# Top-k attention on one core: an exact mask line, a looped exact search, and part of the bound test moved to GpSimd

## The chip, the cores and the metric

The kernel runs on one core of a Trainium2 chip. The core has five engines that run side by side and meet through semaphores: TensorE (PE; its weight loads are shown as PEld), VectorE (DVE), ScalarE (ACT), GpSimd (POOL) and the queue engine SP. The metric is the time of one execution on the device, in microseconds (us), as the median of several runs.

## The reference, cut to what matters

Four layers follow each other on x of shape 32 x 256 x 128: attention a, a mixture of experts, attention b, the experts again. Only attention a is touched. It has 16 heads of width 8, and each query keeps its 76 largest scores of 256:

```python
topk = max(1, int(Tx * 0.3))                       # 76
scores = jnp.einsum('bhid,bhjd->bhij', q, k) * scale
topk_scores, indices = jax.lax.top_k(scores, topk)
masked = jnp.full_like(scores, -jnp.inf)
masked = masked.at[bi, hi, ti, indices].set(topk_scores)
attn = jax.nn.softmax(masked, axis=-1)
out = jnp.einsum('bhij,bhjd->bhid', attn, v)
```

That is 32 x 16 x 256 = 131,072 rows of 256 scores, and in each the 76th largest value has to be found.

## The kernel before, in words

**Groups and steps.** The work of attention a is cut into 64 groups of 8 heads (two groups per sequence). A group is 16 tiles of 128 queries x 256 keys, held in SS, which has room for four groups. The engines run steps: in step t, group t is counted, group t-1 is searched, and groups t-2 and t-3 are masked, turned, exponentiated and weighed. A step has eight slots, one per head. Four steps are unrolled in the body of a hardware loop (`schedule`).

**Finding the 76th value.** ScalarE counts, three times over all 16 tiles, how many scores of a row lie above a threshold (`count`, line 792: an activation with Sign and an accumulator). After each of the first two counts GpSimd moves the threshold (`move`, lines 474 to 476); after the third it writes the upper bound hi_t (line 496) and kk, the place of the wanted value below that bound (line 498). VectorE then, for each head (`largest`, lines 919 to 942), zeroes the values above hi_t (line 928, two operations on two tiles), takes the 8 largest (933), removes them (937) and takes the next 8 (941). That gives 16 sorted values per row, in L. `picks` (lines 944 to 973) reads mid, the value in place kk, and nxt, the one after it.

**The mask line.** The cut is set half-way between mid and nxt, times 1e15 (lines 961 and 966). ScalarE writes relu(cut - 1e15 x score) into gone (`outsiders`, line 768), which is large for what has to go. The two values count as apart only if mid x (1 - 2^-20) is above nxt (line 963).

**The exact search.** A row fails if kk is not in 1 to 15, if the largest value found isn't below the bound, if mid is not positive, or if mid and nxt are not apart. TensorE adds the failures of each tile over its rows (`judged`), and VectorE reads the sums (`check_flags`, lines 990 and 992, in slot 3). If any is over zero, `redo` goes through 16 unrolled copies of a search, one per tile: each reads the flag of its tile, and branches past the copy if it is zero; otherwise ten rounds of MAX8 and MATCH_REPLACE8 run on that tile (lines 1049 to 1055). If none is over zero, one branch goes past all 16 copies. After that VectorE signals okay (line 994).

**What waits for okay.** GpSimd's differences of group t-2 (line 488: scores minus their maximum, scaled, into ring, two tiles for each head), and ScalarE's outsiders of that group. TensorE turns ring and gone together (`turn`, lines 637 and 638), and ScalarE exponentiates the result (line 778).

**GpSimd's own order in a step.** hi_t and kk; differences of heads 6, 7 of group t-3; in even steps the reciprocal deviation of the next sequence; the first move; the wait for okay; differences 0, 1, 2 of group t-2; the second move; in odd steps `guess` (line 454, a power over 32 columns, and lines 456 and 457); differences 3, 4, 5; in even steps a copy of the values (line 517). VectorE evacuates the scores of group t+1 into SS in the same step (`evac`, line 913), takes the sums for the normalisation (`normalise`, line 982), and masks a Gram matrix (line 876).

Of the kernel before, what the change touches and what calls it, by code (L numbers as in the profile page):

```python
# [4 lines left out]
BATCH, T, D = 32, 256, 128  # L5
P = 128
HALVES = T // P
# [48 lines left out]
def build(nc, x, W_qkv, b_qkv, W_out, b_out, Wq, Wk, Wv, Wp, pos, gate_w, gate_bias,  # L56
# [7 lines left out]
    with ctx:  # L64
        def sb(name, shape, dt=f32):
            return ctx.enter_context(nc.sbuf_tensor(name, shape, dt))
# [43 lines left out]
        mlast = sb("mlast", [P, HALVES, 8])  # L110
        nb = sb("nb", [P, 2, HALVES])
        work = sb("work", [P, HALVES, T])
# [221 lines left out]
        zt = ab("zt", [P, 2, T])  # L334
        vraw = ab("vraw", [P, HALVES * H, HD])
# [19 lines left out]
                      "diff out pused pt pv on own aown pown slow oc gate pgate upper vput ini inid")  # L355
# [74 lines left out]
        with nc.Block() as block:  # L430
            @block.gpsimd
            def _(pool):
# [31 lines left out]
                def step(t, b, u):  # L464
# [373 lines left out]
            def _(dve):  # L838
# [55 lines left out]
                def step(t, b, u):  # L894
# [24 lines left out]
                    def largest(lag, p, between):  # L919

                        if not runs(t, lag):
                            return
                        z, y = (u - lag) % 4, (u - lag + 1) % 2
                        if own.n:
                            own.need(own.n)
                        for i in range(2):
                            c = 2 * p + i
                            n = own.mark(V.scalar_tensor_tensor(zt[:, i, :], SS[:, z, c, :], hi_t[:, y, c:c + 1], SS[:, z, c, :],  # L928
                                                                ALU.is_le, ALU.mult))
                        next(between, None)  # L930
                        for i in range(2):
                            own.need(n - 1 + i)
                            m = own.mark(V.max(L[:, y, 2 * p + i, 0:8], zt[:, i, :]))
                        next(between, None)
                        for i in range(2):
                            own.need(m - 1 + i)
                            n = own.mark(V.match_replace(zt[:, i, :], L[:, y, 2 * p + i, 0:8], zt[:, i, :], GONE))
                        next(between, None)
                        for i in range(2):
                            own.need(n - 1 + i)  # L940
                            m = own.mark(V.max(L[:, y, 2 * p + i, 8:16], zt[:, i, :]))
                        next(between, None)

                    def picks():
# [91 lines left out]
                def redo(dve, V, z):  # L1036
# [4 lines left out]
                    with dve.If(any_failed > 0):  # L1041
                        for c in range(GT):
                            failed = dve.value_load(flags[0:1, c:c + 1], min_val=0, max_val=P)
                            with dve.If(failed > 0):
                                slow.n = 0
                                src = SS[:, z, c, :]
                                w = work[:, 0, :]
                                for r in range(TOPK // 8 + 1):
                                    slow.link(V.max(mx[:, 0, :], src if r == 0 else w))
                                    if r == TOPK // 8:  # L1050
                                        slow.link(V.memset(mx[:, 0, TOPK % 8:8], GONE))
                                    slow.link(V.match_replace(w, mx[:, 0, :], src if r == 0 else w, GONE))
                                slow.link(V.tensor_scalar(w, w, GONE_BELOW, -FAR, ALU.is_gt, ALU.mult))
                                slow.link(V.tensor_tensor(src, src, w, ALU.add))
                                slow.link(V.memset(cut[:, z, c:c + 1], -0.5 * FAR * STEEP))
# [812 lines left out]
```

## Time and profile before

| | |
|---|---|
| median of 3 runs | 5771.29 us (5760.17 to 5799.41) |
| profiled execution, its own time | 5762.57 us |
| span of that execution in the trace | 5760.7 us |
| attention a in the trace | about the first 3000 us |
| busy over the span | PE 89%, DVE 72%, ACT 62%, POOL 32% |
| mean granted TensorE clock | 0.889 |

The profile is one execution. A share over the whole span mixes four layers, so the stage has to be read by windows. "Idle before" is time in which the engine ran nothing ahead of an instruction, with what released it: another engine's line, or "issue" where the profile shows no wait. Clock is the granted share of TensorE's full speed.

### The profile page before, as it was taken

What the parts mean: (1) busy time and instruction counts of PE and PEld (TensorE: products, weight loads), DVE (VectorE), ACT (ScalarE), POOL (GpSimd) and SP (SyncE); (2) the same over time, 40 slices, a digit from 0 to 9 for tenths busy, and PEclk for the clock granted to TensorE, in tenths of its full rate; (3) what the DMA queues carried; (4) which work ended last, traced back from release to release, by engine and by line L of the source; (5) the groups of instructions that cost most, each with busy time, mean ns of one, the idle gap of its engine ahead of it and who ended that gap; (6) DMA issues with size and microseconds to landing.
All of it is one profiled execution on the core that took longest, in us unless ns stands there. A gap on an engine that the chain in (4) does not pass through costs nothing. (4 is left out here: it accounts for less than half of the span.)

```text
span 5760.7 us, 127365 instructions
## 1 busy us (share of the span) xinstructions
PE 5131.6 (89%) x36862; PEld 3785.5 (66%) x36862; DVE 4153.1 (72%) x14778; ACT 3573.5 (62%) x11201; POOL 1843.7 (32%) x3026
## 2 busy tenths in 40 slices
PE   5788899899878898999888999989999999899998
PEld 3455566566545565655557888877666667788887
DVE  3777687887777888778867888865555555688886
ACT  3777688888777888888872222227767777222222
POOL 1223232332223233233324444441111111344444
PEclk6677788887788889788889999999999999999999
DMA  2000000000000000000003444430000000334434
GB/s 59 1 1 2 2 2 1 1 2 2 2 2 2 2 2 2 2 2 1 1 1 75 89 83 80 89 61 12 10 12 10 11 10 10 75 76 86 88 75 103
DMA packets 199731, 165.26 MB, mean 29 GB/s; under 512 B 47971, under 2 KB 195974, under 8 KB 199046
## 3 DMA queue, kind: packets, MB, share of 16 engines
q1 hardware_dynamic: 199046, 157.32, 13.4%
q8 instruction: 284, 4.65, 0.3%
q14 instruction: 401, 3.28, 0.2%
HBM read 146.52 MB, written 10.49 MB: 27 GB/s over the span
## 5 line engine op out<-in xcount | busy, mean ns | idle before, releaser
L792 ACT ACTIVATE junk<-SS,nt 128x256 bf16<-128x256 f32 x3072 | 1516.2, 502 | 20.9 <-DVE SS L913 17.5
L1256 ACT ACTIVATE f_th<-bank 128x256 f32<-128x256 f32 x1088 | 416.9, 383 | 1148.5 <-PE bank L1187 1148.5
L1156 POOL TENSOR_TENSOR f_hid<-f_g_m,f_cbs 128x256 f32<-128x256 f32 x1024 | 743.6, 726 | 852.3 <-DVE f_g_m L1401 630.8
L637 PE MATMUL bank<-ident,ring 128*128 128x128 f32 x4096 | 914.2, 350 | 37.8 <-issue 27.6
L637 PEld LDWEIGHTS bank<-ident,ring 128*128 128x128 f32 x4096 | 739.9, 226 | 269.9 <-issue 215.5
L1186 PE MATMUL bank<-f_xTf,wgT 128*128 128x256 f32 x2176 | 693.1, 400 | 52.7 <-DVE f_g_m L1401 39.1
L488 POOL TENSOR_SCALAR ring<-SS,nmx 128x256 f32<-128x256 f32 x1024 | 524.0, 512 | 592.7 <-DVEq L994 438.2
L1802 DVE TENSOR_REDUCE nmxb<-bank 128x2 f32<-128x512 f32 x512 | 329.5, 686 | 476.0 <-PE bank L1574 476.0
L928 DVE SCALAR_TENSOR_TENSOR zt<-SS,hi_t 128x256 f32<-128x256 f32 x1024 | 478.9, 508 | 255.3 <-issue 241.1
L650 PE MATMUL bank<-pT,vaug 128*32 128x256 f32 x2048 | 643.7, 446 | 11.2 <-ACT pT L778 8.5
L1187 PE MATMUL bank<-f_xTf,wuT 128*128 128x256 f32 x2176 | 651.4, 381 | 0.0
L1218 PEld LDWEIGHTS bank<-wdT,f_hid 128*128 128x128 f32 x4096 | 601.5, 191 | 67.3 <-POOL f_hid L1156 13.2
L1218 PE MATMUL bank<-wdT,f_hid 128*128 128x128 f32 x4096 | 629.5, 276 | 10.4 <-POOL f_hid L1156 10.3
L792 ACT ACTIVATION_READ_ACCUMULATOR junk<-SS,nt 128x1 f32 x3072 | 602.2, 196 | 0.0
L768 ACT ACTIVATE gone<-SS,cut 128x256 bf16<-128x256 f32 x1024 | 464.0, 505 | 155.3 <-DVEq L994 130.0
L609 PE MATMUL bank<-k,q 8*128 8x256 f32 x2048 | 531.4, 455 | 19.5 <-DVE SS L913 14.3
L1393 DVE SCALAR_TENSOR_TENSOR f_g_s<-f_th,bank 128x256 f32<-128x256 f32 x1088 | 451.4, 415 | 106.9 <-ACT f_th L1256 87.2
L1401 DVE TENSOR_TENSOR f_g_m<-f_g_s,bank 128x256 f32<-128x256 f32 x1088 | 456.3, 419 | 75.2 <-POOL f_hid L1156 0.4
L638 PE MATMUL bank<-minus,gone 128*128 128x128 bf16 x2048 | 498.4, 243 | 0.0
L1693 ACT ACTIVATE probb<-bank,nmxb 128x256 f32<-128x256 f32 x1024 | 440.5, 494 | 78.1 <-DVE nmxb L1802 77.6
L778 ACT ACTIVATE pT<-bank 128x512 f32<-128x512 f32 x512 | 300.9, 589 | 292.4 <-PE bank L638 291.9
L609 PEld LDWEIGHTS bank<-k,q 8*128 8x128 f32 x2048 | 314.6, 213 | 249.4 <-issue 161.2
(234 smaller groups left out, 8603.2 us busy)
## 6 DMA issues: line engine op xcount, KB each, us to landing
f_cbs<-f_shares SPq DMA_DIRECT2D x512, 256.0 KB, 5.9
qrow<-q_rows SPq DMA_DIRECT2D x512, 8.0 KB
q_rows<-qTb SPq DMA_DIRECT2D x32, 128.0 KB, 2.0
out_dram<-xres SPq DMA_DIRECT2D x4, 1024.0 KB, 9.3
f_shares<-f_combT SPq DMA_DIRECT2D x64, 32.0 KB, 1.5
px<-pext SPq DMA_DIRECT2D x16, 15.8 KB
nat<-in_L_attn_a_W_qkv_dram SPq DMA_DIRECT2D x3, 64.0 KB
bqk<-in_L_attn_a_b_qkv_dram SPq DMA_DIRECT2D x8, 0.1 KB
```

Source lines behind the costliest of these rows:

```text
L488: last = pool.tensor_scalar(ring[:, h % 4, i, :], SS[:, (u - lag) % 4, c, :], nmx[:, (u - lag) % 4, c:c + 1], DOWN, ALU.add, ALU.mult)
L609: last = nc.tensor.matmul(S[h % 3][:, i * T:(i + 1) * T], q4[r, par, g // 4, i * P:(i + 1) * P], k4[r, par, g // 4, :], start=True, stop=True)
L637: nc.tensor.matmul(o, ring[:, h % 4, i, k * P:(k + 1) * P], ident[:, :], start=True, stop=False)
L638: last = nc.tensor.matmul(o, gone[:, h % 4, i, k * P:(k + 1) * P], minus[:, :], start=False, stop=True)
L650: last = nc.tensor.matmul(O[PAD32 * (h % 4):PAD32 * (h % 4 + 1), (h // 4) * T:(h // 4 + 1) * T], vaug4[:, v // 2, k, 8 * (v % 2) + h, :], ...
L768: last = nc.scalar.activation(gone[:, h % 4, i, :], SS[:, v, c, :], ACT.Relu, bias=cut[:, v, c:c + 1], scale=-STEEP)
L792: nc.scalar.activation(junk[:, c % 2, :], SS[:, uu % 4, c, :], ACT.Sign, bias=bias(c), accum_out=acc[:, k, uu % 4, c:c + 1]).then_inc(s["s ...
L928: n = own.mark(V.scalar_tensor_tensor(zt[:, i, :], SS[:, z, c, :], hi_t[:, y, c:c + 1], SS[:, z, c, :], ALU.is_le, ALU.mult))
L1156: pool.tensor_tensor(hid[:, e % NBUF, :], g_m[:, e % NBUF, :], cbs[:, par, e, :], ALU.mult).then_inc(s["hid"], 1)
L1186: nc.tensor.matmul(g[:, 0:T], wgT[:, e, :], xTf[:, par, :], start=True, stop=True)
L1187: nc.tensor.matmul(g[:, T:2 * T], wuT[:, e, :], xTf[:, par, :], start=True, stop=True).then_inc(s["gu"], 1)
L1218: last = nc.tensor.matmul(Y[par][h][:, 0:D], src[:, h * P:(h + 1) * P], wdT[:, e, :], start=(e == 0), stop=(e == NBLK - 1))
```

## The change

Three things are done in attention a.

1. **Mask line.** cut becomes mid x 2^50, and ScalarE's scale -2^50. The two values count as apart if nxt is below mid. One operation on 16 columns of VectorE goes, and the others no longer wait for one another.
2. **Exact search.** The 16 unrolled copies become one copy in a hardware loop over the tiles, with addresses taken from the loop's register. The search gets one copy of the tile ahead of its rounds.
3. **Bound test.** For heads 1, 3, 5, 7 of each group (p odd) GpSimd makes the searched tile, in ztp, by two operations per tile: (score > hi_t) x -1e30, then plus the score. VectorE leaves out line 928 for those heads, waits for trimmed instead, and signals searched when it is done with the buffer. ztp has room for two heads. In GpSimd's order the trims of head 1 come right after hi_t and kk, head 3 after differences 6, 7, head 5 after differences 0, 1, 2, and head 7 after `guess`, ahead of differences 3, 4, 5.

```diff
-        STEEP, FAR, APART = 1.0e15, 1.0e20, 1.0 - 2.0 ** -20
+        STEEP, FAR = 2.0 ** 50, 1.0e20
...
+                    def trims(heads):
+
+                        if not runs(t, 1):
+                            return
+                        for p in heads:
+                            wait(pool, s["searched"], 4 * (t - 1) + (p - 3) // 2)
+                            pool.sem_inc(s["pgate"], 1)
+                            for i in range(2):
+                                c = 2 * p + i
+                                n = own.mark(pool.tensor_scalar(ztp[:, (p // 2 % 2) * 2 + i, :], SS[:, (u + 3) % 4, c, :], hi_t[:, u % 2, c:c + 1], -1.0e30,
+                                                                ALU.is_gt, ALU.mult))
+                            for i in range(2):
+                                c = 2 * p + i
+                                own.need(n - 1 + i)
+                                last = pool.tensor_tensor(ztp[:, (p // 2 % 2) * 2 + i, :], ztp[:, (p // 2 % 2) * 2 + i, :], SS[:, (u + 3) % 4, c, :], ALU.add)
+                            last.then_inc(s["trimmed"], 1)
...
+                    trims((1,))
                     differences(3, (6, 7))
+                    trims((3,))
...
                     differences(2, (0, 1, 2))
+                    trims((5,))
                     if runs(t):
                         move(1, "u2", nt[:, 0, :], nt[:, 1, :])
                     if not even and ahead:
                         guess(bb + 1, (par + 1) % 2)
+                    trims((7,))
                     differences(2, (3, 4, 5))
...
+                        if p % 2 == 0:
+                            x = zt[:, 0:2, :]
...
+                        else:
+                            x = ztp[:, (p // 2 % 2) * 2:(p // 2 % 2) * 2 + 2, :]
+                            wait(dve, s["trimmed"], 4 * (t - lag) + p // 2 + 1)
+                            dve.sem_inc(s["gate"], 1)
...
-                        between = own.mark(V.tensor_tensor(cut[:, z2, :], nxt[:, :], mid[:, z2, :], ALU.add))
-                        own.need(between)
-                        apart = own.mark(V.scalar_tensor_tensor(nxt[:, :], mid[:, z2, :], APART, nxt[:, :], ALU.mult, ALU.is_gt))
+                        own.mark(V.tensor_scalar(cut[:, z2, :], mid[:, z2, :], STEEP, None, ALU.mult))
+                        apart = own.mark(V.tensor_tensor(nxt[:, :], nxt[:, :], mid[:, z2, :], ALU.is_lt))
                         yield
                         own.need(apart)
-                        own.mark(V.tensor_scalar(cut[:, z2, :], cut[:, z2, :], 0.5 * STEEP, None, ALU.mult))
...
-                        for c in range(GT):
-                            failed = dve.value_load(flags[0:1, c:c + 1], min_val=0, max_val=P)
+                        with dve.Fori(0, GT) as c:
+                            failed = dve.value_load(flags[0:1, bass.ds(c, 1)], min_val=0, max_val=P)
                             with dve.If(failed > 0):
...
+                                slow.link(V.tensor_copy(w, src))
                                 for r in range(TOPK // 8 + 1):
-                                    slow.link(V.max(mx[:, 0, :], src if r == 0 else w))
+                                    slow.link(V.max(mx[:, 0, :], w))
```

## Rows read from the trace of the kernel before

**Rows 1.** The page, part 1 (busy us, share, instructions) and the granted clock in 40 slices

```profile
...
PE 5131.6 (89%) x36862; PEld 3785.5 (66%) x36862; DVE 4153.1 (72%) x14778; ACT 3573.5 (62%) x11201; POOL 1843.7 (32%) x3026
...
PEclk6677788887788889788889999999999999999999
...
```

**Rows 2.** Length, busy us of PE, PEld, DVE, ACT, POOL, clock: 59 steps, three quiet ones

```profile
...
254.20:2917.40 2663.20, 2317.49 (x11500) 1529.65 (x11498) 2105.11 (x8221) 2183.21 (x7526) 810.94 (x1600) 0.81 0.01 2
...
2067.70:2108.00 40.30, 38.35 (x194) 25.33 (x192) 34.49 (x136) 34.92 (x123) 10.01 (x19) 0.82 0.01 2
2108.00:2153.00 45.00, 41.19 (x201) 27.36 (x200) 34.83 (x137) 38.42 (x132) 16.81 (x35) 0.82 0.01 3
2153.00:2192.00 39.00, 32.43 (x188) 21.54 (x186) 34.91 (x136) 38.32 (x134) 12.97 (x22) 0.96 0.01 2
...
```

**Rows 3.** The same view, summed over the five steps from 385 us on that search

```profile
...
sum 334.20, PE 204.88 PEld 135.53 DVE 232.70 ACT 182.36 POOL 66.42; mean PE 40.98 PEld 27.11 DVE 46.54 ACT 36.47 POOL 13.28
```

**Rows 4.** Waits from 254.2 to 2917.4 us: engine, line, releaser; us in total, times, longest

```profile
...
ACT pT L778 <- PE bank L638: 250.5, 137, 6.0
DVE zt L928 <- issue: 227.7, 59, 8.4
...
ACT gone L768 <- DVEq L994: 107.5, 5, 28.2
...
PE bank L590 <- DVE gram L876: 99.4, 14, 31.9
...
PE bank L674 <- DVE onrm L982: 47.2, 25, 2.8
ACT q L741 <- PE bank L553: 43.9, 29, 2.2
...
```

**Rows 5.** Line 1055, the last operation of each exact search, in the whole program

```profile
...
L1055 DVE MEMSET cut<- x7: 59/59/59, 234.7 to 1878.6; 128x1 f32 x7
...
```

**Rows 6.** VectorE in order of time, [idle before], around a search from 1525 us

```profile
...
1525.87 0.43 DVE L1049 MAX8 mx<-SS 128x8 f32<-128x256 f32 x1 [7.90 <-issue]
...
1544.02 1.10 DVE L928 SCALAR_TENSOR_TENSOR zt<-SS,hi_t 128x256 f32<-128x256 f32 x2 [7.31 <-issue]
```

**Rows 7.** VectorE in order of time around a search from 1867 us

```profile
...
1867.86 0.43 DVE L1049 MAX8 mx<-SS 128x8 f32<-128x256 f32 x1 [13.22 <-issue]
...
1880.87 1.10 DVE L928 SCALAR_TENSOR_TENSOR zt<-SS,hi_t 128x256 f32<-128x256 f32 x2 [2.16 <-issue]
...
```

**Rows 8.** GpSimd in order of time, 2150 to 2200 us

```profile
...
2172.45 0.20 POOL L474 TENSOR_SCALAR shift<-acc 128x16 f32<-128x16 f32 x1 [8.33 <-ACT junk L792]
...
2185.47 0.20 POOL L474 TENSOR_SCALAR shift<-acc 128x16 f32<-128x16 f32 x1 [6.22 <-ACT junk L792]
...
2186.35 5.46 POOL L454 TENSOR_TENSOR sig<-var,half_p 128x32 f32<-128x32 f32 x1
...
2192.86 3.60 POOL L488 TENSOR_SCALAR ring<-SS,nmx 128x256 f32<-128x256 f32 x6 [0.30 <-POOL nt L457]
2199.38 0.41 POOL L496 TENSOR_SCALAR hi_t<-nt 128x16 f32<-128x16 f32 x1 [2.93 <-ACT junk L792]
...
```

**Rows 9.** VectorE in order of time, 2160 to 2181 us, a quiet step

```profile
...
2164.31 0.16 DVE L961 TENSOR_TENSOR cut<-nxt,mid 128x16 f32<-128x16 f32 x1
2164.51 0.18 DVE L963 SCALAR_TENSOR_TENSOR nxt<-mid,nxt 128x16 f32<-128x16 f32 x1
...
2168.04 0.87 DVE L928 SCALAR_TENSOR_TENSOR zt<-SS,hi_t 128x256 f32<-128x256 f32 x2
...
2175.56 1.10 DVE L928 SCALAR_TENSOR_TENSOR zt<-SS,hi_t 128x256 f32<-128x256 f32 x2 [3.61 <-issue]
...
```

**Rows 10.** The page, part 5: a GpSimd operation on two SBUF tiles in the experts

```profile
...
L1156 POOL TENSOR_TENSOR f_hid<-f_g_m,f_cbs 128x256 f32<-128x256 f32 x1024 | 743.6, 726 | 852.3 <-DVE f_g_m L1401 630.8
...
```

**Rows 11.** TensorE in order of time, 2180 to 2200 us

```profile
...
2188.33 0.49 PE L674 MATMUL bank<-woT,oT 128*128 128x128 f32 x2 [2.70 <-DVE onrm L982]
...
2197.58 0.49 PE L637 MATMUL bank<-ident,ring 128*128 128x128 f32 x2
...
```

More of the change, by code:

```diff
@@ L109, in build @@
         mx = sb("mx", [P, HALVES, 8])
-        mlast = sb("mlast", [P, HALVES, 8])
-        nb = sb("nb", [P, 2, HALVES])
-        work = sb("work", [P, HALVES, T])
+        work = sb("work", [P, T])
         gone = sb("gone", [P, 4, HALVES, T], bf16)
@@ L334, in build @@
         zt = ab("zt", [P, 2, T])
+        ztp = ab("ztp", [P, 4, T])
         vraw = ab("vraw", [P, HALVES * H, HD])
@@ L354, in build @@
         s = sems("a", "mv rstd xn m0 m0c m1 m1c var sig scores evac signs u0 u1 u2 thr failed flag okay "
-                      "diff out pused pt pv on own aown pown slow oc gate pgate upper vput ini inid")
+                      "diff out pused pt pv on own aown pown slow oc gate pgate upper vput trimmed searched ini inid")
         S = bank[0:3]
@@ L925, in largest @@
                             own.need(own.n)
-                        for i in range(2):
-                            c = 2 * p + i
-                            n = own.mark(V.scalar_tensor_tensor(zt[:, i, :], SS[:, z, c, :], hi_t[:, y, c:c + 1], SS[:, z, c, :],
-                                                                ALU.is_le, ALU.mult))
+                        if p % 2 == 0:
+                            x = zt[:, 0:2, :]
+                            for i in range(2):
+                                c = 2 * p + i
+                                n = own.mark(V.scalar_tensor_tensor(x[:, i, :], SS[:, z, c, :], hi_t[:, y, c:c + 1], SS[:, z, c, :],
+                                                                    ALU.is_le, ALU.mult))
+                        else:
+                            x = ztp[:, (p // 2 % 2) * 2:(p // 2 % 2) * 2 + 2, :]
+                            wait(dve, s["trimmed"], 4 * (t - lag) + p // 2 + 1)
+                            dve.sem_inc(s["gate"], 1)
+                        next(between, None)
+                        for i in range(2):
+                            if p % 2 == 0:
+                                own.need(n - 1 + i)
+                            m = own.mark(V.max(L[:, y, 2 * p + i, 0:8], x[:, i, :]))
+                        next(between, None)
+                        for i in range(2):
+                            own.need(m - 1 + i)
+                            n = own.mark(V.match_replace(x[:, i, :], L[:, y, 2 * p + i, 0:8], x[:, i, :], GONE))
                         next(between, None)
@@ L932, in largest @@
                             own.need(n - 1 + i)
[L933 to L941, printed above, removed]
+                            m = own.mark(V.max(L[:, y, 2 * p + i, 8:16], x[:, i, :]))
+                        if p % 2 == 1:
+                            own.need(m)
+                            dve.sem_inc(s["searched"], 1)
                         next(between, None)
@@ L1041, in redo @@
                     with dve.If(any_failed > 0):
[L1042 to L1043 removed]
+                        with dve.Fori(0, GT) as c:
+                            failed = dve.value_load(flags[0:1, bass.ds(c, 1)], min_val=0, max_val=P)
                             with dve.If(failed > 0):
                                 slow.n = 0
[L1046 to L1047 removed]
+                                src = SS[:, z, bass.ds(c, 1), :].rearrange("p a t -> p (a t)")
+                                w = work[:, :]
+                                slow.link(V.tensor_copy(w, src))
                                 for r in range(TOPK // 8 + 1):
[L1049 removed]
+                                    slow.link(V.max(mx[:, 0, :], w))
                                     if r == TOPK // 8:
                                         slow.link(V.memset(mx[:, 0, TOPK % 8:8], GONE))
[L1052 removed]
+                                    slow.link(V.match_replace(w, mx[:, 0, :], w, GONE))
                                 slow.link(V.tensor_scalar(w, w, GONE_BELOW, -FAR, ALU.is_gt, ALU.mult))
                                 slow.link(V.tensor_tensor(src, src, w, ALU.add))
[L1055 removed]
+                                low = cut[:, z, bass.ds(c, 1)]
+                                slow.link(V.tensor_scalar(low, low, 0.0, -0.5 * FAR * STEEP, ALU.mult, ALU.add))
                                 dve.sem_clear(s["slow"])
```

## The prediction

> **What bounds the kernel now.** I read the page first, for where the engines are busy and how the clock runs: the granted clock is 0.6 to 0.9 in the first half, which is attention a, and 1 behind it [rows 1]. Only that half is touched, so I cut it into steps and read busy time by windows [rows 2]. From 254.2 to 2917.4 us there are 59 steps, counted by VectorE's idle time behind the flags, which comes once a step [rows 4]. In 2663.2 us ScalarE is busy 2183.2, 37.0 a step, and no other engine keeps so close to the step in its quietest form: in the step from 2153 us, clock 0.96, ScalarE is busy 38.3 of 39.0 us and VectorE 34.9. The two steps ahead of it take 40.3 and 45.0 us with the clock at 0.82, and there TensorE is busy 38.4 and 41.2 us [rows 2].
>
> Five of the 59 steps are long, 334.2 us together [rows 3]; the other 54 take (2663.2 - 334.2) / 54 = 43.1 us each. I call these quiet.
>
> Then the waits tell what ScalarE lacks [rows 4]. It waits for TensorE's turned tiles 250.5 us and for its projections 43.9, together 5.0 a step, and 107.5 us in five pieces for okay, which are the five long steps. It waits for VectorE in no other place. But TensorE waits for VectorE: 99.4 us for gram and 47.2 for onrm. One such wait is in the quietest step, 2.70 us at 2188 us [rows 11]. So the order is: **ScalarE sets the pace, its idle time comes through TensorE, and a part of that comes from a late VectorE.**
>
> VectorE's own step: 34.9 us busy, 3.61 us idle behind the flags without a wait [rows 9], 38.5 of 39.0. So in a quiet step at full clock VectorE and ScalarE are the bound together.
>
> **Part 1, the mask line, and what it does to searches.** On VectorE it takes away one operation of 0.16 us and one dependent wait (line 961 starts at 2164.31, line 963 0.20 later) [rows 9]: 0.2 us a step.
>
> The larger effect is on the number of searches. There were 7 tiles searched [rows 5]. Which test failed, the trace doesn't show. I worked the reference's own inputs through the kernel's counts in float32. One row of 131,072 ends with kk outside 1 to 15 (group 1, tile 13). The rest of what comes near failing are pairs mid, nxt that lie within some 2^-20 of one another. Among them are group 5 tiles 4 and 10, group 9 tile 9, group 29 tile 7 and group 30 tile 6, and those are groups that are searched in the long steps. The idle times fit the tiles: 7.90 us ahead of the search and 7.31 behind it for tile 7 [rows 6], 13.22 and 2.16 for tile 13 [rows 7], so (13.22 - 7.90) / 6 = 0.89 us per tile passed. Six rows in some 131,072 within 2^-20 make about half a row of exact equality, whose distance is a tenth of that. I expect one search or two to be left, not 7.
>
> Five long steps at 66.8 instead of 43.1 us are 23.7 x 5 = 118 us; the sixth, whose search ends at 234.7 us [rows 5], is the row of group 1 and stays. From below: if none of the searches goes, nothing; from above: six steps, 142 us. I take all five: **-118 us**.
>
> **Part 2, the loop.** Where nothing failed, VectorE's queue went past 16 copies of the search, idle 3.61 us [rows 9]. Past one copy, with a flag read, it was 0.89 us [rows 6, 7]. The loop is about one copy and a few instructions long, so the idle time lies between 0.9 and 3.6 us; I take 1.2, because the distance branched is that of the near row. That is -2.4 us a step on VectorE, and okay comes as much earlier.
>
> The Trainium skill (Runtime: NRT & Kernel Launch, Instruction fetch mechanics) says that a taken branch out of the pages held on the engine waits for a fetch; the rows at 0.89 and 3.61 us agree, and by it too the looped form pays no fetch.
>
> Where a search is left, 16 turns of the loop cost at least the 0.89 x 15 of before, plus the loop's own end, a copy of 0.4 us, and perhaps as much again: +0 to +15 us per searched step. I take **+8**.
>
> **Part 3, the bound test.** VectorE loses line 928 for four heads: a pair is 0.87 us [rows 9], so 3.5 us a step. It gains two semaphore instructions per head, priced at 0.1 a head: net -3.1.
>
> GpSimd gains, per head, two operations of one SBUF tile (line 488: six in 3.60 us, 0.60 each [rows 8]) and two of two tiles (line 1156: 0.726 us [rows 10], with issue 0.8): 1.2 + 1.6 = 2.8 us, 11 a step, on 13 busy of 39 [rows 2]. It has the room; the question is the order. In the odd step from 2153 us, behind the second move at 2185.47, there is guess, then the ring from 2192.86, and then 2.93 us idle before hi_t at 2199.38 [rows 8]. The trims of head 7 fill 2.8 of these 2.93. Head 3's ring, the first two operations of that stretch, comes 2.8 us later, at 2192.86 + 2.8 + 1.2 = 2196.9; TensorE turned it at 2197.58 [rows 11]. Both fit with under 1 us to spare. Ahead of the second move GpSimd is idle 6.22 us, room for head 5's 2.8; ahead of the first it is idle 8.33 us, room for the 5.6 us of heads 1 and 3 [rows 8]. Priced at nothing in even steps, at 0 to 1 us in odd ones.
>
> While GpSimd works, VectorE's two-input pair stretches from 0.87 to 1.10 us [rows 9]. Two of four remaining pairs so: +0.5 us on VectorE. The Trainium skill (GPSIMD Engine Reference, Key points) says that GpSimd shares SBUF interfaces with VectorE and that both contend where VectorE has two SBUF inputs. If every remaining pair met the new two-input operations and took as long again, it would be about 3.5 us a step instead of 0.5.
>
> **The sum.** VectorE's step falls from 38.5 to 38.5 - 0.2 - 2.4 - 3.1 + 0.5 = 33.3 us. ScalarE's work stays at 37.0. So VectorE leaves the bound, and what is gained is only what ScalarE waits. It waits 43.1 - 37.0 = 6.1 us in a quiet step. Bounds: TensorE's waits for gram and onrm, 146.6 us / 59 = 2.5 a step, are what a late VectorE can put into them; nothing is the lower bound, all 6.1 the upper. I take 2.8: those waits and a little of okay's. 64 x 2.8 = **-180 us**. What is late next is TensorE at its lower clock, which a faster VectorE doesn't help.
>
> Together 5762.6 - 118 + 8 - 180 = 5473 us. The median of the runs is 8.7 us above the profiled execution, 0.15%; I predict 5475.
>
> **Rivals.**
> 1. *Clock gives back as well.* All quiet steps come down to ScalarE's work and a few tenths, 37.6 us, because TensorE without waits for VectorE keeps the higher of its two levels (2.4 against 1.2 GHz). For it: the step at 0.96 is the shortest. Against it: with a ScalarE bound, TensorE waits more for ScalarE. 5762.6 - 110 - 64 x 5.5 = 5301 us. Chance 0.16.
> 2. *Only the searches.* ScalarE's waits come from TensorE at 1.2 GHz, not from VectorE, and stay: 40.3 and 45.0 us at 0.82 [rows 2]. 5762.6 - 110 = 5653, say 5650 us. Chance 0.14.
> 3. *The searches stay* (another test fails, or rounding makes equal pairs): the change to the mask doesn't do what it seems. 5762.6 - 180 + up to 6 x 8 = 5630 us; with the branch at 3.6 us too, 5690. Chance 0.10.
> 4. *GpSimd's order takes it back*, the slower end. The place is head 7's trims behind guess: they decide once GpSimd needs over 2.93 us for them [rows 8], or TensorE wants head 3's ring before 2196.9. Then ring and hi_t are late in each odd step, and the step grows by the 2.8 us plus the clock that falls: the neighbour at 0.82 takes 6 us more than that at 0.96 [rows 2]. 32 x 8.8 = 282 against 110 of the searches gives 5762.6 + 172 = 5935 us; with half of that stretch 5794. Against it: GpSimd has 26 us idle of 39. Chance 0.10, half of it within 1%.
>
> **How the numbers follow.** My forecast has 0.50, its own range 5400 to 5560. Down to 5340 it takes in most of rival 1, up to 5655 rival 2 and most of rival 3, which leaves out under 0.2. A change within 1% (5714 to 5829 us) is what a measurement of this kernel can't tell from none. Faster: 0.50 + 0.16 + 0.14 + 0.10 = 0.90. Same 0.05, slower 0.05.
>
> **What would show it.** Searched tiles: 1 or 2 in place of 7. Idle time behind the flags near 1.2 us. VectorE busy 31 to 32 us a quiet step, GpSimd 22 to 24. ScalarE still 37.0 busy, its waits for TensorE down from 5.0 to some 2.5 a step, TensorE's waits for onrm and gram nearly gone. VectorE now waits, for hi_t or for scores. It is wrong if ScalarE begins to wait for GpSimd, if TensorE's wait for ring grows past 1 us in odd steps, or if the mean clock of the stage falls below 0.81.

## The result and the profile after

| | median, us | range, runs | ratio to before, 95% |
|---|---|---|---|
| before | 5780.5 | 5760.2 to 5799.4, 4 | |
| changed | 5965.9 | 5957.3 to 5966.4, 4 | 1.036 (1.031 to 1.041) |

The changed kernel is 3.6% slower. The forecast was 5475 us, faster at 0.9, with a range up to 5655: it was wrong in sign and size. The profiled execution took 5965.6 us. Some executions of one kernel run over 1.5% above its fastest, at a lower granted clock; the ratios here and below leave those out, the medians don't.

The page after: part 1, the granted clock in 40 slices, and two groups of part 5 (busy us, mean ns of one, idle time ahead). Line 500 is the first half of a trim, line 487 is the old line 488.

```profile
PE 5225.3 (88%) x36862; PEld 3842.1 (64%) x36862; DVE 3985.2 (67%) x14035; ACT 3580.6 (60%) x11201; POOL 2791.9 (47%) x4050
...
PEclk6687788887887788787789999999999999999999
...
L500 POOL TENSOR_SCALAR ztp<-SS,hi_t 128x256 f32<-128x256 f32 x512 | 595.7, 1163 | 78.9 <-POOL kk L514 23.7
...
L487 POOL TENSOR_SCALAR ring<-SS,nmx 128x256 f32<-128x256 f32 x1024 | 504.4, 493 | 345.8 <-DVEq L1022 233.1
```

Against [rows 1], VectorE lost 168 us of work, ScalarE and TensorE kept theirs within 2%, and GpSimd gained 948 us where the prediction priced 64 x 11.2 = 717. The clock digits of attention a are much like those of before.

Windows of the changed kernel: length, then busy us (count) of PE, PEld, DVE, ACT, POOL, the clock, DMA share and GB/s. The first is the first experts stage, then an odd step, the even step behind it, and 59 steps of attention a.

```profile
3125.80:4060.60 934.80, 827.81 (x4571) 714.67 (x4572) 645.57 (x2347) 233.06 (x633) 396.43 (x573) 0.94 0.34 73
2174.50:2210.50 36.00, 32.38 (x198) 21.80 (x197) 33.07 (x126) 35.83 (x126) 25.58 (x40) 1.00 0.01 2
2210.50:2266.40 55.90, 46.88 (x197) 30.32 (x195) 33.31 (x130) 39.12 (x133) 33.93 (x53) 0.69 0.00 1
258.50:2947.00 2688.50, 2322.49 (x11304) 1529.92 (x11302) 1915.21 (x7399) 2151.51 (x7394) 1653.00 (x2495) 0.80 0.01 1
```

The same experts stage before:

```profile
3045.70:3854.90 809.20, 781.78 (x4571) 686.73 (x4572) 645.39 (x2347) 232.46 (x633) 396.38 (x573) 1.00 0.42 83
```

Three things are to be seen. The experts stage, of which no line was changed, takes 125.6 us more with the same work on VectorE, ScalarE and GpSimd. The odd step is quicker than any of [rows 2]; the even one behind it takes 55.9 us at clock 0.69. And the 59 steps, which [rows 2] has at 2663.2 us, are longer although one of them holds a search where five did. In the profiled executions the first experts stage begins at 3125.8 us instead of 3045.7, so **the slowdown of 203 us has two parts: 80 us in attention a, 126 us in the first experts stage** (the rest gives back 3).

The waits of the 59 steps (us in all, times, longest), to be read against [rows 4]:

```profile
ACT pT L798 <- PE bank L658: 348.2, 168, 6.0
PE bank L657 <- POOL ring L487: 149.0, 29, 6.3
DVE xn L883 <- POOL rstd L448: 121.2, 29, 4.2
DVE SS L933 <- POOL ring L487: 106.9, 28, 6.4
DVE zt L950 <- issue: 29.7, 23, 2.7
ACT gone L788 <- DVEq L1022: 22.0, 1, 22.0
PE bank L694 <- DVE onrm L1010: 20.8, 16, 1.4
```

ScalarE's wait for okay has gone from five long pieces to one, TensorE's for onrm from 47.2 to 20.8 us, and its wait for gram, 99.4 us before, no longer shows. In their place GpSimd is waited for: ring by TensorE and by VectorE, rstd (the reciprocal deviation) by VectorE, each some 28 times, which is once in every second step.

### The profile page after: what moved, and what is told of

Read it like the earlier page. It is cut to its first block and busy times, and to the rows that moved or that the text cites. A ratio compares the mean times of both kernels' runs of the same rounds, so it can differ in the third digit from the quotient of the medians.

```text
span 5963.9 us, 128647 instructions
## 1 busy us (share of the span) xinstructions
PE 5225.3 (88%) x36862; PEld 3842.1 (64%) x36862; DVE 3985.2 (67%) x14035; ACT 3580.6 (60%) x11201; POOL 2791.9 (47%) x4050
## 5 line engine op out<-in xcount | busy, mean ns | idle before, releaser
L657 PE MATMUL bank<-ident,ring 128*128 128x128 f32 x4096 | 940.8, 357 | 191.1 <-POOL ring L487 160.6
L657 PEld LDWEIGHTS bank<-ident,ring 128*128 128x128 f32 x4096 | 758.6, 231 | 428.1 <-issue 261.2
L1216 PE MATMUL bank<-f_xTf,wgT 128*128 128x256 f32 x2176 | 710.9, 409 | 130.9 <-DVE f_g_m L1431 114.1
L487 POOL TENSOR_SCALAR ring<-SS,nmx 128x256 f32<-128x256 f32 x1024 | 504.4, 493 | 345.8 <-DVEq L1022 233.1
L1217 PE MATMUL bank<-f_xTf,wuT 128*128 128x256 f32 x2176 | 665.1, 388 | 0.0
L500 POOL TENSOR_SCALAR ztp<-SS,hi_t 128x256 f32<-128x256 f32 x512 | 595.7, 1163 | 78.9 <-POOL kk L514 23.7
L1423 DVE SCALAR_TENSOR_TENSOR f_g_s<-f_th,bank 128x256 f32<-128x256 f32 x1088 | 451.1, 415 | 222.0 <-issue 104.7
L629 PE MATMUL bank<-k,q 8*128 8x256 f32 x2048 | 549.6, 466 | 29.2 <-issue 18.2
L933 DVE TENSOR_SCALAR_CACHE_REDUCE SS<-bank 128x256 f32<-128x256 f32 x1024 | 388.1, 416 | 186.0 <-POOL ring L487 112.5
```

The costliest lines, as they stand in the source:

```text
L500: n = own.mark(pool.tensor_scalar(ztp[:, (p // 2 % 2) * 2 + i, :], SS[:, (u + 3) % 4, c, :], hi_t[:, u % 2, c:c + 1], -1.0e30, ALU.is_gt, ...
L629: last = nc.tensor.matmul(S[h % 3][:, i * T:(i + 1) * T], q4[r, par, g // 4, i * P:(i + 1) * P], k4[r, par, g // 4, :], start=True, stop=True)
L657: nc.tensor.matmul(o, ring[:, h % 4, i, k * P:(k + 1) * P], ident[:, :], start=True, stop=False)
L1216: nc.tensor.matmul(g[:, 0:T], wgT[:, e, :], xTf[:, par, :], start=True, stop=True)
L1217: nc.tensor.matmul(g[:, T:2 * T], wuT[:, e, :], xTf[:, par, :], start=True, stop=True).then_inc(s["gu"], 1)
L1423: n = own.mark(V.scalar_tensor_tensor(g_s[:, e % 3, :], th[:, e % 3, :], 1.0, g[:, 0:T], ALU.add, ALU.mult))
```

## Experiments

"Quiet step" below is the mean over the steps of the stage without a search, odd and even apart, with the cut of [rows 2]; `guess` begins at the end of an odd step, so what stands behind it falls into the even one. "Experts" is the first experts stage. The kernel before has medians from 5755 to 5781 us in the different sessions; the ratios are each against its runs on the same chip. A difference of two medians of different sessions is good to some 25 us and more. The steps and stages are those of one profiled execution each; 10's took 5836.6 us, 37 over its median, and its steps are left out.

| | median us | ratio, 95% | odd / even step | clock | experts |
|---|---|---|---|---|---|
| before | 5780.5 | | 39.9 / 46.6 | .88 / .80 | 809 |
| changed | 5965.9 | 1.036 (1.031-1.041) | 37.3 / 54.9 | .92 / .73 | 935 |
| 1 mask and loop | 5631.9 | 0.976 (0.969-0.983) | 37.7 / 49.0 | .90 / .77 | 809 |
| 2 ring 3 first | 5896.6 | 1.024 (1.018-1.030) | 36.1 / 53.9 | | 934 |
| 3 heads 1, 3, 5 | 5734.1 | 0.996 (0.993-1.000) | 36.9 / 51.1 | | 808 |
| 4 trims only | 5884.8 | 1.022 (1.016-1.028) | 38.5 / 51.2 | | 811 |
| 5 changed, 20 waits | 5825.6 | 1.014 (1.006-1.021) | 37.2 / 54.4 | | 809 |
| 6 mask, loop, 20 waits | 5789.3 | 0.999 (0.994-1.004) | 37.0 / 46.5 | | 952 |
| 7 trims for nothing | 5804.6 | 1.009 (1.006-1.012) | 38.7 / 52.3 | | 810 |
| 8 the same, cheaper | 5775.0 | 1.003 (0.999-1.007) | 38.1 / 51.1 | | 808 |
| 9 new order, 20 waits | 5660.5 | 0.985 (0.978-0.992) | 36.8 / 48.8 | .92 / .78 | 808 |
| 10 mask only | 5799.3 | 1.007 (1.002-1.012) | | | 954 |
| 11 loop only | 5762.6 | 1.002 (0.998-1.006) | 37.3 / 48.3 | | 808 |
| 12 mask, loop, products | 5554.8 | 0.965 (0.958-0.972) | 36.5 / 46.3 | .98 / .86 | 807 |
| 13 changed, 20 waits, products | 5754.9 | 0.998 (0.994-1.001) | 35.6 / 53.0 | 1.0 / .78 | 808 |
| 14 new order, products | 5575.7 | 0.967 (0.961-0.974) | 35.8 / 47.1 | 1.0 / .85 | 808 |
| 15 twelve products | 5624.6 | 0.975 (0.969-0.982) | 37.0 / 47.5 | .99 / .89 | 809 |

### Which part: mask and loop alone, trims alone

Experiment 1 is the change without its third part; experiment 4 is the third part alone, with seven unrolled searches. 10 and 11 split the first: the mask line alone, and the loop alone.

> Parts 1 and 2 alone: the exact mask line and the looped search, all heads' bound test back on VectorE. Theory A (the trims of head 7, ahead of the rings of heads 3 to 5 in GpSimd's order, make TensorE wait and its clock fall) and theory B (the trims' load on GpSimd costs wherever it stands): no wait for ring, five searches fewer, 1 us instead of 3.6 behind the flags: 5580 us, 5520 to 5650. Theory C (the loop or the mask line is what costs, the trims are hidden): 5850 us or more.

> Part 3 alone: GpSimd's trims as in the changed kernel, with the mask line and the 16 unrolled searches of before. Theories A and B: the loss of the trims with 7 searched tiles on top and 3.6 us behind the flags: 6100 us, 6020 to 6200. Theory C: 5700 to 5800 us.

> Part 1 alone, the unrolled search kept. My own step: five searches fewer, five long steps of 66.8 us become 43.1: attention a ends 118 us earlier, near 2840 us in the trace; 3.6 us behind the flags stays. Rival: the searches stay at 7 and nothing moves. The experts' loop begins at instruction 9529, 57 past a multiple of 256; by theory D (slow at 50 and 54, quick at 34, 46, 69, 70 and 85) the first experts stage is slow, 935 us, and the whole 5771 - 118 + 126 = 5779 us.

> Part 2 alone, the old mask line kept: 7 tiles searched in the looped form at 8 us more in each of 6 steps, +48 us, and 1.0 instead of 3.6 us behind the flags. If that idle time was on the path: -2.6 x 64 = -166 us, whole 5650 us. If it only sends TensorE into a slower clock in even steps (as with parts 1 and 2 together): no gain, 5820 us. Loop of the experts at 46 past: quick.

Mask and loop gain 134 us by the medians, inside the expected range. Trims alone lose 2.2%, 119 us; they came out at 5885 us where 6020 to 6200 was expected. The mask alone shows 1.007 (5799 us, 5779 forecast), but its experts stage is 145 us longer than before; without that it stands at about 5650 us, a gain of some 105 us against its own session's before, most of which is the long steps that are gone. The loop alone shows no change of the whole, 1.002, between the two forecasts of 5650 and 5820. Its six searched steps are 31 us longer together than those of before in the profiles, so its quiet steps must have given back about as much (42.8 against 43.3 us, odd and even in the mean): some half a microsecond a step, of 2.4 taken off VectorE.

The same sum for experiment 1: four long steps gone are 95 us and the looped form costs 5 in each of the two left, so some 50 us of the 134 are left for the quiet steps, 0.9 a step of the 2.8 forecast. Its profile shows none of it, but that is its slowest execution; experiment 6, the same kernel moved by 20 instructions, shows 1.5 a step. So **part three loses, and of what is taken off VectorE little comes back.** The trims cost 119 us on the kernel before and 194 on experiment 1; why the two differ stays open. Two quiet steps of experiment 1, odd and even, and the stretch from 300 to 2700 us:

```profile
1939.50:1981.80 42.30, 35.78 (x198) 24.35 (x195) 34.68 (x137) 39.38 (x138) 18.35 (x35) 0.92 0.01 1
...
2106.00:2159.50 53.50, 48.47 (x198) 30.86 (x195) 34.72 (x136) 39.69 (x138) 18.30 (x35) 0.68 0.00 1
...
300.00:2700.00 2400.00, 2184.90 (x10647) 1437.27 (x10646) 1897.89 (x7408) 2016.93 (x6958) 741.41 (x1467) 0.81 0.01 1
```

The same work on every engine takes 42.3 us at clock 0.92 and 53.5 at 0.68, where TensorE is busy 48.5 of them. VectorE and ScalarE are busy under 40 us in both, and what differs is TensorE's time, partly at its lower level (1.2 GHz). That TensorE sets such a step is read from this pair; the experiments with products below test it.

### Where the trims stand

```diff
 # 2: head 3's ring ahead of head 7's trims
+                    differences(2, (3,))
                     trims((7,))
-                    differences(2, (3, 4, 5))
+                    differences(2, (4, 5))
 # 3: head 7 stays on VectorE
-                    trims((7,))
 # 9: as 2, and the reciprocal deviation (front) ahead of the first trims; 20 waits as in 5
+                    if even and ahead:
+                        front(bb + 1)
                     trims((1,))
                     differences(3, (6, 7))
                     trims((3,))
-                    if even and ahead:
-                        front(bb + 1)
```

> The changed kernel with one move in GpSimd's order: head 3's difference ahead of head 7's trims, heads 4 and 5 behind them. Theory A: head 3's ring is 4 us earlier, TensorE's 6 us wait at each even step's start is gone, and the clock with it: 5480 us, 5400 to 5600. Theory B: the load is the same, so 5900 us or more.

> The changed kernel with head 7's trims off GpSimd, VectorE does that head's bound test as before. Theory A: as with the move, no wait for ring: 5480 us, 5400 to 5600. Theory B: a quarter of the load goes, so a quarter of the loss against parts 1 and 2 alone: about 5870 us.

> The changed kernel with both late things moved ahead in GpSimd's order: the reciprocal deviation ahead of all trims, head 3's difference ahead of head 7's trims; and with the 20 waits that keep the first experts stage at 809 us. Theory A (order): no wait for ring, none for the deviation, so the even steps are no longer than without trims (49 us) and VectorE's relief counts on top: 5600 us, 5520 to 5660. Theory B (any 4.0 us block in GpSimd's queue or the load itself delays something): 5750 us or more.

The change itself, GpSimd in order of time (start, duration, [idle before]) where an odd step ends:

```profile
2207.55 5.45 POOL L453 TENSOR_TENSOR sig<-var,half_p 128x32 f32<-128x32 f32 x1
...
2214.11 2.39 POOL L500 TENSOR_SCALAR ztp<-SS,hi_t 128x256 f32<-128x256 f32 x2 [0.36 <-POOL nt L456]
2216.58 1.41 POOL L505 TENSOR_TENSOR ztp<-ztp,SS 128x256 f32<-128x256 f32 x2
2218.08 3.32 POOL L487 TENSOR_SCALAR ring<-SS,nmx 128x256 f32<-128x256 f32 x6
2221.49 0.27 POOL L512 TENSOR_SCALAR hi_t<-nt 128x16 f32<-128x16 f32 x1
```

TensorE and VectorE at the same place:

```profile
2219.17 0.80 PE L657 MATMUL bank<-ident,ring 128*128 128x128 f32 x2 [5.92 <-POOL ring L487]
```

```profile
2219.41 0.42 DVE L933 TENSOR_SCALAR_CACHE_REDUCE SS<-bank 128x256 f32<-128x256 f32 x1 [4.56 <-POOL ring L487]
...
2233.74 0.60 DVE L883 TENSOR_SCALAR xn<-xres,mv,rstd 128x128 f32 x2 [4.18 <-POOL rstd L448]
...
2239.86 1.10 DVE L950 SCALAR_TENSOR_TENSOR zt<-SS,hi_t 128x256 f32<-128x256 f32 x2 [1.01 <-DVE flags L1020]
```

The trims of head 7 take 4.0 us (2214.11 to 2218.08) where 2.93 were free [rows 8], and hi_t now begins without idle time ahead of it. Head 3's ring is 5.9 us late for TensorE, and VectorE, which can't put new scores into SS before the ring has read the old ones, is late by 4.6. Fifteen microseconds on, the reciprocal deviation comes behind two heads' trims, and VectorE waits 4.2 us for it; behind that xn stand the next projections, on TensorE.

Experiment 2 moves only the ring. It came out at 5896.6 us, not at 5480. Its waits from 300 to 2700 us:

```profile
DVE xn L884 <- POOL rstd L448: 151.0, 26, 6.0
PE bank L567 <- DVE xn L884: 110.3, 25, 8.5
PE bank L658 <- POOL ring L487: 36.0, 17, 2.3
```

The wait for ring falls to 2.3 us at most, but that for rstd rises from 4.2 to 6.0, and TensorE then waits for xn. With its own experts stage put at 808, experiment 2 stands near 5771, 55 us under experiment 5. Experiment 9 moves both:

```profile
ACT pT L799 <- PE bank L659: 179.3, 104, 6.0
PE bank L658 <- POOL ring L487: 38.6, 18, 2.4
PE bank L567 <- DVE xn L886: 14.2, 8, 2.4
```

That gives 5660.5 us (at the edge of the 5520 to 5660 expected) against 5825.6 with the same trims and the same 20 instructions: **165 us of the 194 that the trims cost inside attention a are their place in GpSimd's order.** TensorE's wait for ring, 38.6 us, is back near the 33.2 of experiment 1, and VectorE's for rstd is gone. What stays above experiment 1 is 29 us by the medians and some 50 by the ratios, whose intervals overlap. VectorE's relief didn't count on top, as theory A had it. No run moves the deviation alone. Experiment 3, without head 7's trims, is 92 us under experiment 5; at 5734 us it lies between its two forecasts, 5480 and 5870.

### What they cost by themselves

Experiments 7 and 8 are the mask and loop, and GpSimd does the trims in their places for nothing: VectorE does all its work as before and waits for none of them. 8 has another first operation:

```diff
-                                                                ALU.is_gt, ALU.mult))
+                                                                ALU.add, ALU.mult))
```

> Parts 1 and 2 alone, and GpSimd does the trims of part 3 at their places for nothing: VectorE neither waits for them nor reads them, and does every bound test itself. Theory A (GpSimd's order delays ring and the reciprocal deviation): the waits return without VectorE's waits for trimmed, even steps near 55 us, 5632 + 200 = 5830 us. Theory E (VectorE's waits for trimmed tiles and the way it signals are what costs): about 5632 us.

> As the one before, but with an addition in the place of the comparison in the first operation of the trims (the result isn't used). Theory F (the comparison's 1163 ns, where I had 478 to 600, is what tips the order): 2.8 us a head instead of 4.0, nearly as without trims, 5632 to 5700 us. If the order fails even at the price I predicted: 5770 us or more.

They cost 173 and 143 us over experiment 1; all of their ten executions each are slower than the slowest of its four, as theory A and the second forecast for 8 had it. The two operations of experiment 8 by line (busy us, mean ns, idle before):

```profile
L499 POOL TENSOR_SCALAR ztp<-SS,hi_t 128x256 f32<-128x256 f32 x426 | 215.2, 505 | 57.7 <-POOL kk L513 15.2 <-POOL nt L456 7.8 <-POOL nt L475 5.6
...
L504 POOL TENSOR_TENSOR ztp<-ztp,SS 128x256 f32<-128x256 f32 x425 | 317.8, 768 | 17.1
```

That is 2 x 0.505 + 2 x 0.768 = 2.55 us a head, less than the 2.8 predicted, and it still costs 143 us. So the price of is_gt, 1163 ns in place of the 600 taken from line 488, is worth some 30 us of the time; the rest would have come at the predicted price. But it isn't the same wait: from 300 to 2700 us VectorE waits for rstd 94.1 us in experiment 7 and 4.0 in 8, TensorE for ring 90.9 and 42.7 (33.2 in experiment 1). The waits for GpSimd are nearly those of experiment 1, and where the 143 us come from stays open. And the change's VectorE, relieved of 3.5 us a step, brings nothing back: 194 us of loss with the relief, 173 without it, 5825.6 against 5804.6 in one session.

### The stage behind

Experiments 5 and 6 put 20 waits that are always met into VectorE's program ahead of attention a, in the changed kernel and in experiment 1.

```diff
+                for _ in range(40):
+                    dve.wait_ge(s["ini"], 3)
```

(Every second one is merged away when the program is built.)

> The changed kernel with 20 more instructions on VectorE ahead of attention a's loop (waits on a semaphore that is long satisfied). They do nothing but move all later VectorE instructions. The first experts stage, which the change doesn't touch, took 934.8 us in the changed kernel and 809.2 before, with 104 us of VectorE idle on issue. Theory D (its loop of 272 instructions has come to lie badly in VectorE's instruction stream): that stage is back at 809 us, the whole 5840 us. Theory B' (GpSimd's load or the data layout reaches into the experts): it stays at 935 us, the whole 5967 us.

> Parts 1 and 2 alone, again with 20 more waits on VectorE. Without them the experts' loop begins at instruction 2594 of the built program and is quick; in the changed kernel it begins at 2610 and is slow; in the kernel with heads 1, 3, 5 at 2606 and quick. With them it begins at 2614. Theory D: now this kernel is the slow one, first experts stage 935 us, the whole 5632 + 126 = 5758 us. Theory B': 5632 us, as the load on GpSimd is that of before.

The first experts stage of experiment 5, then that of experiment 6 with VectorE's wait in it:

```profile
3104.10:3913.20 809.10, 781.48 (x4571) 686.42 (x4572) 645.84 (x2347) 232.42 (x633) 396.49 (x573) 1.00 0.38 83
```

```profile
2865.40:3816.90 951.50, 838.68 (x4571) 723.47 (x4572) 644.72 (x2347) 233.57 (x633) 396.34 (x573) 0.93 0.33 71
```

```profile
DVE f_g_s L1396 <- issue: 94.6, 14, 7.2
```

Twenty instructions that do nothing take the stage's 126 us away from one kernel and put 142 on the other; both were forecast. The whole of experiment 6 is less clean than its stage: its ten executions took 5717 to 5843 us (experiment 1: 5599 to 5674), and the profiled one, among the quickest, has an attention a some 88 us shorter than experiment 1's profile with the same operations, at a clock of 0.93 and 0.82 (odd and even steps) against 0.90 and 0.77. In the changed kernel the same wait is 104.7 us in 22 pieces, up to 7.1 long, on line 1423 (the same line, shifted), and TensorE waits behind it:

```profile
DVE f_g_s L1423 <- issue: 104.7, 22, 7.1
...
PE bank L1216 <- DVE f_g_m L1431: 95.8, 101, 5.1
```

So **126 us of the slowdown is the length of VectorE's program ahead of this loop, not its content.** The loop is 272 instructions long on VectorE. By the count of instructions ahead of it in the program as built, modulo 256, it begins at 50, 54 or 57 in the kernels where the stage is slow (changed and 2; 6; 10), and at 34, 46, 69, 70 or 85 in all others. The Trainium skill (Runtime: NRT & Kernel Launch, Instruction fetch mechanics) says that an engine holds two pages of 256 instructions and that a branch out of them waits for a fetch. By it a loop of 272 fits into two pages from all but 15 of 256 places, and the slow ones would lie in one band of 15; the positions found agree. The count's zero need not be that of the pages, so where the band lies is read from the runs and not forecast. The traces agree on the fetch: the queue that brings instructions moves 78 packets in the slow stage of the changed kernel, and 8 in the same stage of experiment 5:

```profile
q14 instruction: 78, 0.64, 0.3%
```

```profile
q14 instruction: 8, 0.07, 0.0%
```

(packets, MB, share of the DMA engines.) It is 78 in experiments 6 and 10 as well, and 8 in the kernel before and in experiment 1. In the changed kernel the second experts stage, the same lines at another place in the program, has no such wait.

### Is it the clock, and does VectorE matter once the clock is held?

TensorE gets six products of a constant with itself (twelve in 15) ahead of each head's turn, where it would wait; nobody reads them. TensorE's wait for pt moves ahead of its two others with them; no run makes that move alone.

```diff
+                        wait(pe, s["pt"], 8 * g + h - 1)
+                        for _ in range(6):
+                            nc.tensor.matmul(PT[h % 2][:, 0:P], minus[:, :], minus[:, :], start=True, stop=True)
                         wait(pe, s["diff"], 8 * g + h + 1)
                         wait(pe, s["out"], 8 * g + h + 1)
-                        wait(pe, s["pt"], 8 * g + h - 1)
```

> Parts 1 and 2 alone, and TensorE does six extra 128x128 bf16 products ahead of each head's turn, while it would wait for ring and gone; they are overwritten. Theory G (the even steps are long because TensorE drops to 1.2 GHz after short waits and then is the bound): the clock stays near 1, even steps come from 49 to 41 us, whole 5400 us, 5330 to 5500. Rival (the waits themselves, or TensorE's own work, set the steps): 8 x 6 x 0.1 us more work a step, 5700 us or more.

> The changed kernel with the 20 waits, and TensorE's six extra products ahead of each turn. Theory G (the clock is most of what the trims cost): even steps from 54.4 to under 48 us, whole 5826 down to 5600 us. Rival (the wait for ring, 5.1 us, and for the deviation, 4.2 us, are lengths of their own on the chain): even steps 52 us, whole 5740 us or more.

> The reordered trims (deviation first, head 3's ring first), the 20 waits, and the extra products. If the clock is held, VectorE's relief of 3 us a step either shows against the 5555 us without trims: 5450 us; or ScalarE and TensorE set the steps and it shows nothing: 5540 to 5600 us.

> Parts 1 and 2 alone with twelve extra products ahead of each turn instead of six. Theory G: the even steps, still at 0.86 of the clock with six, come up further: 5480 us. Rival: twelve are 8 x 12 x 0.06 = 5.8 us of TensorE a step at full clock and more than its idle time: 5600 us or more.

From 300 to 2700 us, experiments 12, 13 and 14:

```profile
300.00:2700.00 2400.00, 2202.44 (x13972) 1524.61 (x13971) 2000.69 (x7803) 2121.13 (x7338) 790.63 (x1550) 0.91 0.01 2
```

```profile
PE bank L659 <- POOL ring L487: 108.9, 27, 5.9
...
DVE xn L887 <- POOL rstd L448: 108.6, 26, 4.2
...
300.00:2700.00 2400.00, 2137.33 (x13008) 1476.59 (x13009) 1754.04 (x6818) 1986.03 (x6834) 1539.27 (x2298) 0.86 0.01 2
```

```profile
ACT pT L801 <- PE bank L661: 86.0, 54, 4.7
...
300.00:2700.00 2400.00, 2186.82 (x13959) 1515.33 (x13956) 1873.92 (x7320) 2117.78 (x7322) 1656.75 (x2463) 0.91 0.01 2
```

Experiment 12 raises the clock from 0.81 to 0.91 and gains 77 us on experiment 1 (63 by the ratios; its slowest execution, 5573 us, is under the quickest of experiment 1): at **5554.8 us, ratio 0.965, it is the best version found** (14, at 0.967, isn't told apart from it). Theory G had expected 5400 us, three times that gain. It makes the clock the likely cost of the even steps. Two other readings agree: experiment 6 has even steps of 38.0 us at clock 1.00 and of 52.0 at 0.67, ScalarE busy 36.6 and 37.1; and of 25 executions of the kernel before in one session the quickest took 5708 us at a clock of 0.900 and the slowest 5792 at 0.881.

In the changed kernel (13) the clock rises to 1.0 in odd steps, but in even ones only from 0.73 to 0.78, and the waits for ring and rstd stay at 4 us in the mean, once each per two steps: 53.0 us in the even steps, 71 us gained in all, as the rival had it. The products didn't hold the clock there, so how the loss divides between the waits and the clock behind them isn't shown. Experiment 14, the new order with products, has VectorE relieved, TensorE's waits for ring at 1.7 us at most, the clock as high as in 12, ScalarE's wait for TensorE at 86 us, and is no quicker than 12, as one of its two forecasts said; VectorE waits 43.6 us for trimmed tiles in it. Twelve products are worse than six, at a clock as good or better, as the rival said; that TensorE's own added work is the reason was not measured by itself.

## Why the prediction was wrong, step by step

- **Searches, -118: nearly right.** Seven went to two, as said: that of group 1, and one more. The second lies in the last of the five long steps of [rows 3], so four of them went, 4 x 23.7 = 95 us. An operation near the end of each search in the changed kernel, with its count and the first and last time:

```profile
L1083 DVE TENSOR_TENSOR SS<-SS,work x2: 425/426/426, 237.6 to 1877.9; 128x256 f32 x2
```

- **The loop: right, +8 included.** Idle time behind the flags is 1.0 to 1.3 us where 1.2 was taken. With the loop alone (experiment 11) the six searched steps are longer by 31 us together, 5 each. Around the second search of the changed kernel VectorE is idle 17.0 and 2.7 us where [rows 7] has 13.22 and 2.16; that step takes 77.1 us where the unrolled one took 66.8, and 73.2 with the loop alone:

```profile
1867.32 0.29 DVE L1076 COPY work<-SS 128x256 f32 x1 [17.00 <-issue]
...
1881.37 1.10 DVE L950 SCALAR_TENSOR_TENSOR zt<-SS,hi_t 128x256 f32<-128x256 f32 x2 [2.73 <-issue]
```

- **VectorE's step, 38.5 to 33.3: about right.** It is busy 1915.2 / 59 = 32.5 us a step (31 to 32 said). It was the next sentence that failed: "So VectorE leaves the bound, and what is gained is only what ScalarE waits", priced at 2.8 us a step, **-180 us. By the medians the runs show some 50 us of it,** not far above their scatter. Odd and even quiet steps take 43.35 us in the mean in the profile of experiment 1 (its slowest execution) and 41.75 in that of experiment 6, against 43.25 before. Two things were wrong. I had picked the quietest step of [rows 2] as the one that shows the bound. The mean is made by the others, and there TensorE was busy 38.4 of 40.3 us, at clock 0.82. And 2.5 of the 2.8 were TensorE's waits for gram and onrm over all 59 steps. Three pieces of the wait for gram, 31.9, 21.6 and 21.1 us at 446, 651 and 1548 us, stand in long steps, whose whole excess was already in the -118: 74.6 of 146.6 us were counted twice. The rest mostly went away in the changed kernel and in experiment 1, and little time came back with it: in experiment 1 there are shorter odd steps (39.9 to 37.7) and longer even ones (46.6 to 49.0) at a clock lower by 0.03. Rival 2 had the mechanism for parts one and two. That its 5653 lies so near 5632 is partly luck: it counted one long step too many, 24 us, and no gain in the quiet ones.
- **Trims "Priced at nothing in even steps, at 0 to 1 us in odd ones": wrong, and the step that turned the sign.** It cost 194 us in attention a. "Both fit with under 1 us to spare" rested on 2.8 us a head. They took 4.0, and the margin of 0.13 in 2.93 was gone. What I left out was the instruction behind the first trims: the reciprocal deviation, in even steps, named in my own account of GpSimd's order and then not followed to its reader. I had counted GpSimd's idle time (8.33 us) as room and not asked who waits for the work behind it. With the order put right 165 of the 194 us are gone. The wrong price is not the whole of it: at 2.55 us a head (experiment 8) the wait for the deviation is 4.0 us in all and that for ring nearly the one without trims, and yet 143 us are lost; what makes these is not known. Rival 4 had the right place for one half, "behind guess", the right decision point (over 2.93 us) and a size close by accident: its 5935 priced the loss at 282 us in attention a, where 194 and an unrelated 126 to 140 came together.
- **VectorE stretched by GpSimd, +0.5: a little low.** From 300 to 2700 us the operation of line 928 takes 619 ns in the mean in the changed kernel (line 950 there) and 507 before, eight in a step: 0.9 us, far from the 3.5 of the worst case. It has little weight where VectorE sets few of the steps.
- **Everything behind attention a was priced at nothing by silence.** 126 us of the 203 in the profiles are there. No row of before could give it a size, but that VectorE's program gets shorter by some 7000 instructions was in the diff.
- **The signs I gave for being wrong held:** TensorE's wait for ring over 1 us, and the clock at 0.80, under 0.81 (by too little to count). GpSimd's 1653 / 59 = 28.0 busy us a step (22 to 24 said) are the mis-sized is_gt.

By medians of several sessions the account is: mask and loop -134, trims in attention a +194, experts stage +140 (126 in the profiles), together +200; measured +185 by the medians, +208 (177 to 239) by the ratio. The three terms are differences along one row of kernels and so add up by themselves; that they agree with the whole checks only the scatter between sessions.

## What to carry to other kernels

Idle time on an engine is room only for work behind which nothing urgent is queued: for each place of insertion, write down the next instruction of that queue and the first reader of its result. Read the bound off the steps that make up the mean, not off the quietest; where the same step takes 42 and 53 us at two mean clocks, suspect the engine that the clock slows before the others. Don't price a wait that lies in a stretch which another term has already taken away. And before a change is judged, look at the stages that it doesn't touch, and shift the program by some idle instructions if one of them moved.

## What was not expected of the hardware

- GpSimd's two-step operation on a 128 x 256 tile costs 1163 ns with (is_gt, mult) and 493 to 512 with (add, mult); the form of the row taken for a price has to match in its operations too.
- A hardware loop of 272 instructions on one engine takes 808 or 935 to 954 us for the same work, by where it begins in the program, with 8 or 78 packets on an instruction queue. Twenty instructions more decide, in both directions.
- Six unread products per head, more work for TensorE, the engine with the largest busy share, made the kernel 77 us faster, with the granted clock of the even steps 0.86 in place of 0.77; twelve gave 0.89 and took back 70 of these.
